# One PSUM bank given to the output projection, one taken from P·V

## The reference

```
q, k, v = x @ Wq.T, x @ Wk.T, x @ Wv.T      # 16 query heads, 4 key/value heads, 64 wide
s = 30 * tanh(q k / 8 / 30)                 # soft cap
s = where((j <= i) & (j > i - 1024), s, -1e30)
o = softmax(s) v
x = layernorm(x + o @ Wo.T)
W1q, W2q = ternary(W1), ternary(W2)         # clip(round(W / (mean|W| + 1e-5)), -1, 1)
x = layernorm(x + relu(x @ W1q.T + b1) @ W2q.T + b2)
```

## Time and profile before

| | |
|---|---|
| median of 3 runs | 2266.94 us (2266.53 to 2274.94) |
| profiled execution | 2279.37 us, span of its slowest core 2277.8 us |
| cores in it | 2239.8 to 2277.8 us |
| TensorE matmul | 1393.7 us busy, 61% of the span |
| weight load | 750.5 us, 33% |
| VectorE | 582.1 us, 26% |
| ScalarE | 758.9 us, 33% |
| GpSimd | 217.6 us, 10% |
| HBM | 161.53 MB read, 35.65 MB written |

### The profile page before, as it was taken

One profiled execution on the slowest core, in us unless ns is written; L12 is line 12 of the kernel. 1 busy time (PEld: TensorE's weight loads), 2 busy tenths in 40 slices (PEclk: granted clock), 3 DMA queues, 4 the chain that ended last, 5 costly groups with the idle time before them and its releaser, 6 DMA issues. The chain is left out here.

```text
span 2277.8 us, 24033 instructions; the slowest of 8 cores (2239.8 to 2277.8 us)
## 1 busy us (share of the span) xinstructions
PE 1393.7 (61%) x8196; PEld 750.5 (33%) x8196; DVE 582.1 (26%) x759; ACT 758.9 (33%) x682; POOL 217.6 (10%) x261
## 2 busy tenths in 40 slices
PE   3970277755656545655556555159547779947771
PEld 2430155533333333333333333024212224413220
DVE  0234244433322233223322335230011110011211
ACT  1320388844454434444444441023100003311000
POOL 1000000000000000000000001100520000042303
PEclk9995577756656566556666567579877778869775
DMA  9666433221111111111111112522312202233220
GB/s 148 168 184 199 129 94 88 71 74 56 56 42 56 56 58 46 50 61 56 58 40 56 61 47 70 157 89 78 116 43 86 74 33 65 61 120 129 74 92 37
DMA packets 128598, 186.69 MB, mean 82 GB/s; under 512 B 11104, under 2 KB 95072, under 8 KB 124384
## 3 DMA queue, kind: packets, MB, share of 16 engines
q1 hardware_dynamic: 105936, 133.24, 19.2%
q0 software_dynamic: 22544, 51.91, 8.2%
HBM read 161.53 MB, written 35.65 MB: 87 GB/s over the span
## 5 line engine op out<-in xcount | busy, mean ns | idle before, releaser
L536 ACT ACTIVATE Tst<-spsP 128x1024 f32<-128x1024 f32 x256 | 262.2, 1024 | 422.0 <-PE spsP L527 392.9
L519 PE MATMUL spsP<-QT,KTd 64*128 64x128 bf16 x2304 | 226.1, 282 | 140.3 <-ACT Tst L536 136.3
L1035 PE MATMUL f2ps<-hT,w2b 128*128 128x512 bf16 x1024 | 289.2, 453 | 4.4 <-DMA w2b<-w2q_t 3.3
L989 PE MATMUL f1ps<-x2bf,w1b 128*128 128x512 bf16 x1024 | 248.4, 411 | 69.0 <-DVE x2bf L946 68.5
L611 DVE RECIPROCAL den_sb<-pvd 128x256 f32<-128x256 f32 x64 | 112.5, 1757 | 675.6 <-PE pvd L595 662.8
L675 PE MATMUL wops<-OTn,wo_bf 128*128 128x256 bf16 x512 | 108.9, 385 | 284.0 <-DVE r1f L696 284.0
L555 ACT ACTIVATE Pst<-Tst,cm 128x4608 bf16<-128x4608 f32 x64 | 264.8, 4137 | 13.5 <-ACT Tst L542 13.4
L519 PEld LDWEIGHTS spsP<-QT,KTd 64*128 64x128 bf16 x2304 | 122.5, 117 | 242.2 <-issue 236.8
L579 PE MATMUL pvd<-Pst,Vv 128*64 128x256 bf16 x1152 | 194.4, 407 | 0.0
L989 PEld LDWEIGHTS f1ps<-x2bf,w1b 128*128 128x128 bf16 x1024 | 106.3, 104 | 210.7 <-issue 151.6
L1035 PEld LDWEIGHTS f2ps<-hT,w2b 128*128 128x128 bf16 x1024 | 115.8, 113 | 177.6 <-issue 118.7
(11 more groups left out here) (77 smaller groups left out, 940.1 us busy)
## 6 DMA issues: line engine op xcount, KB each, us to landing
qin<-w1T SPq DMA_DIRECT2D x64, 512.0 KB, 4.5
qin<-w2T SPq DMA_DIRECT2D x64, 512.0 KB, 3.8
w2b<-w2q_t SPq DMA_DIRECT2D x32, 1024.0 KB, 4.9
w1b<-w1q_t SPq DMA_DIRECT2D x64, 256.0 KB, 2.6
w1q_t<-qout POOLq DMA_DIRECT2D x32, 256.0 KB, 4.7
xr<-xctxT SPq DMA_DIRECT2D x64, 128.0 KB, 4.1
r1d<-r1f POOLq DMA_DIRECT2D x64, 128.0 KB, 3.9
w2q_t<-qout POOLq DMA_DIRECT2D x32, 256.0 KB, 4.2
```

The costliest lines, as they stand in the source:

```text
L519: sp=last_in_bank: e.matmul(ps[:, col:col + 128], lhsT, rhs, start=st, stop=sp),
L536: lambda e, ps=ps, kbp=kbp: e.activation(Tst[:, kbp * 1024:(kbp + 1) * 1024], ps[:, 0:1024], AF.Tanh, scale=1.0 / 240.0),
L989: lambda e, dc=dc, nt=nt, wslot=wslot, pslot=pslot: e.matmul(f1ps[pslot][:, :], w1b[wslot][:, dc * 128:(dc + 1) * 128], x2bf[:, dc * 1024 ...
L1035: lambda e, fc=fc, nt=nt, wslot=wslot, pslot=pslot: e.matmul(f2ps[pslot][:, :], w2b[wslot][:, fc * 128:(fc + 1) * 128], hT[:, fc * 1024 + ...
```

## The change

The two pvd banks become one, and the bank that this frees goes to wops, so that alternate units of the projection have a bank each (columns 0 to 255 of it). The waits follow: stage A of unit u waits for the reading of u-2 in place of u-1, and P·V of step g waits for the normalisation of g-1 in place of g-2. No instruction is added, removed or moved.

```diff
-                pvd = [p2.enter_context(nc.psum_tensor(f"pvd{i}", [128, 512], F32))
-                       for i in range(2)]
-                wops = p2.enter_context(nc.psum_tensor("wops", [128, 512], F32))
+                pvd = p2.enter_context(nc.psum_tensor("pvd", [128, 512], F32))
+                wopsb = [p2.enter_context(nc.psum_tensor(f"wops{i}", [128, 512],
+                                                         F32)) for i in range(2)]
...
                 def emit_pv(g):
-                    pd = pvd[g % 2]
+                    pd = pvd
...
-                                if g >= 2 and norm_done.get(g - 2, 0) > 0:
-                                    w0.append(("V", norm_done[g - 2]))
+                                if g >= 1 and norm_done.get(g - 1, 0) > 0:
+                                    w0.append(("V", norm_done[g - 1]))
...
                 def emit_norm(g):
-                    pd = pvd[g % 2]
+                    pd = pvd
...
                 def wo_stageA(u):
-                    wreg = (u % 2) * 256
+                    wop = wopsb[u % 2]
...
-                            if u >= 1:
-                                w.append(("V", evac_V[u - 1]))
+                            if u >= 2:
+                                w.append(("V", evac_V[u - 2]))
...
-                                 wops[:, wreg:wreg + 256],
+                                 wop[:, 0:256],
...
                 def wo_stageB(u):
-                    wreg = (u % 2) * 256
...
-                    S.do("vector", lambda e, u=u, wreg=wreg: e.tensor_tensor(
-                        r1f[u % 2][:, :], wops[:, wreg:wreg + 256],
+                    S.do("vector", lambda e, u=u: e.tensor_tensor(
+                        r1f[u % 2][:, :], wopsb[u % 2][:, 0:256],
```

More of the change, by code:

```diff
@@ L670, in wo_stageA @@
                             w.append(("GW", wo_gd[0]))
-                            if u >= 1:
-                                w.append(("V", evac_V[u - 1]))
+                            if u >= 2:
+                                w.append(("V", evac_V[u - 2]))
                         S.do("tensor",
                              lambda e, jc=jc, hc=hc, k=k, half=half,
-                             wreg=wreg: e.matmul(
-                                 wops[:, wreg:wreg + 256],
+                             wop=wop: e.matmul(
+                                 wop[:, 0:256],
                                  wo_bf[:, jc * 1024 + hc * 128:
```

## The result

The changed kernel takes 1919.83 us in the median of 10 runs (1913.14 to 1940.45), the kernel before 2264.15 us beside it. The ratio is 0.848, with a 95% interval of 0.846 to 0.849: 344 us less, where 350 were forecast from 2266.9. The profiled execution took 1919.59 us.

What follows compares the result with a forecast made beforehand. The prediction took TensorE's wait at L675 for a late VectorE read to bound the kernel; 319 + 21 + 5 + 5 = 350 us off 2266.9 gave a median of 1917 us, range 1882 to 1985.

Steps and rivals of the forecast that it cites:

- What bound the kernel: At L675 the projection unit waits for its predecessor's read, queued on VectorE behind the same step's work: 284.0 us.
- Ordinary steps: 40 loop steps with projection and no statistics: 19.48 to 11.5 us each, gain 319 us, bounds 237 and 347.
- The low end of the step: Ordinary step with P·V wholly at the high clock: 36 matmuls take 4.0 us, the step 10.8 us.
- Statistics steps: Five loop steps holding stage D: 26.8 to 22.5 us each, gain 21 us; the 7.54 us stop at L720 stays.
- P·V in one bank: P·V waits for the previous step's normalisation: costs nothing in the loop, cover 3.7 us, up to 3.1 a step without.
- g = 63: After the last loop step P·V has no scores as cover and waits for the normalisation; gain 5 us, not nearly 8.
- Tail: 17 projection units behind the loop, holding 17.8 us of waits: gain 5 us, bounds 0 and 17.8.
- The sum: Whole kernel: 319 + 21 + 5 + 5 = 350 us gained, median 1917 us.
- The low clock: Rival: the clock stays low in ordinary steps, 12 to 13.55 us each; 1937 to 2002 us, chance 0.21.
- the exposed normalisation: Rival: P·V stands still for the normalisation in all 63 steps, 3.1 us each; 2112 us, chance 0.02.
- another wait in ordinary steps: Rival: a new wait replaces the old, such as the statistics matmul for VectorE's squares; about 2055 us, chance 0.04.
- The high clock: Rival: the clock rises and ordinary steps fall under 11 us; 1870 to 1897 us, chance 0.12.

Runs made afterwards that it cites:

- e2: Changed kernel with its two projection banks, but each unit again waits for the reading of u-1: 2264.5 us, ratio 1.001 to before.
- e3: Kernel before, banks unchanged, with stage B of unit u-1 put on VectorE ahead of the normalisation and quantisation: 1922.0 us, ratio 0.850.
- e8: Kernel before, old banks, with stage B and stage D's reading part moved on VectorE ahead of the normalisation: 1882.3 us, ratio 0.832.
- e10: e8 plus five matmuls that nobody reads ahead of each of score pieces 2, 3 and 4: 1820.6 us, ratio 0.804.
- e7: Changed kernel with stage B and stage D's reading part moved on VectorE ahead of the normalisation: 1878.4 us, ratio 0.830.
- e1: Kernel before with P·V in one bank alone, projection keeping its one bank and old wait: 2262.2 us, ratio 1.003.
- e5: Changed kernel with one reciprocal more, 1.9 us, in each normalisation: 1935.9 us, ratio 0.855 to before.
- e6: Changed kernel with three reciprocals more, 5.6 us, in each normalisation: 2093.5 us, ratio 0.925 to before.
- the fillers: Matmuls that nobody reads, put into e8's gaps between score pieces: three a gap 1825.6 us, five a gap 1820.6 us.

## Why the prediction was right

*What bound the kernel.* Right, and shown by e2 and e3: the wait at L675 for a read queued behind the work of the same step.

*Ordinary steps.* Forecast 11.5 us each, measured 11.68; 40 x (19.48 - 11.68) = 312 us where 319 were forecast. The mean clock of 0.74 carried over from the early steps was the right choice between the two ends, the stage has 0.75. The early step plus a unit plus a statistics matmul comes within 0.2 us of the step. That the two stages would share their clock was assumed, and there is luck in it: in e8, with the same ordinary step, the 17 early steps have 0.75 and the long stage 0.79.

*The low end of the step was wrong*, though the forecast did not rest on it. I put P·V at the high clock at 36 x 0.111 = 4.0 us and the step at 10.8 at the least. e10 has P·V in 3.0 us and steps of 9.76: the price of a projection matmul, with its 128 columns of weights, is not that of a P·V matmul with 64. With e10's P·V the sum would have been 5.6 + 3.0 + 1.2 = 9.8, which is about where ScalarE binds.

*Statistics steps.* Forecast 22.5 us each and 21 us of gain, measured 22.1 and 134.0 - 110.7 = 23 us. The stop for stage D stayed, as forecast; e7 shows that it was to be had, 8.5 us in each of five steps.

*P·V in one bank.* Costed at nothing with 3.7 us of cover. e1 shows nothing at steps of 19.5 us, the pairs e3 and changed, e8 and e7 nothing at 11.7, the trace 3.4 us of cover, e5 that 1.9 us more fits into it, e6 that 5.6 does not. At g = 63 the wait came as forecast, 1.93 us, and the step went from 15.8 us (1368.95 to 1384.77) to 11.9 (1036.13 to 1048.01): 3.9 us, 5 forecast.

*Tail.* From the last P·V to the last reciprocal of stage D 57.0 us before and 53.1 now: 3.9 us, 5 forecast. What follows next there is, as expected, VectorE's three operations and the transfers of xr and r1f.

*The sum.* 334.9 us in the 46 steps, 3.9 and 3.9: 342.7 us, against 344 in the medians. The profiled executions differ by 359.8, because the slowest core of before was 19 us slower in the feed-forward stage (836.1 us against 817.0 behind the last statistics), at a clock of 0.77 against 0.79; I had carried 12.4 us of that over as spread, and it did not come back. The start and the 17 early steps differ by 2 us between the two slowest cores. That the median came within 3 us of the 1917 forecast is partly luck: the sum of 350 was 6 us too large, and the 2266.9 that it was taken from was 3 us above the 2264.15 measured with ten runs.

*The rivals.* The low clock did not come, nor the exposed normalisation, nor another wait in ordinary steps. The high clock did not come by itself; it took the fillers. The rival that was put beside a section of the Trainium skill (TensorE: Matmul & The Clock Gate, on psum-queue depth-cycling), a clock that swings as matmul groups cycle through banks with small idles between, is half in the trace: the clock swings, 0.75 on average, but it did so before the projection began. The mean of the long stage rose from 0.61 because the wait went, and not by the number of banks: e3 has 0.76 in its long stage with the old banks, e2 0.61 with the new ones.

## What to carry to other kernels

Where an engine waits for a short read of a buffer, look at what stands ahead of that read in its own engine's order, and when that could begin; a second buffer and an earlier place in the order cure the same wait, and the order costs no memory. Before taking a second buffer away, measure the time between the end of its use and the next write, and what must happen in it: here 6.8 us against 3.1. Removing the wait here also gave back what the low clock behind it cost, and steps of the same kernel that never had the wait told about how much.

## What the hardware showed that I had not expected

In e8 the ordinary steps of 11.7 us have three idle stretches of 0.5 to 0.9 us between score pieces, and the mean granted clock of the long stage is 0.79. With five matmuls that nobody reads in each of them it is 0.95, and the kernel is 62 us faster than e8 although TensorE does more. Whether another way of making the scores dense would do the same was not tried.

The 36 P·V matmuls of 256 columns and 64 weight columns take 3.0 us at the high clock, 0.08 us each, where projection matmuls of 256 columns take 0.11 each (1.04 us for 8, the last one's 0.27 of latency taken off). P·V's two halves go to different output partitions (0 to 63 and 64 to 127), and the timeline shows matmuls of L579 and L595 in turn for a while in the middle of each P·V; whether the halves run side by side was not measured by itself.
